# Query and key projections of one attention layer as seven block products in place of eight

## The reference

```
q = hidden_states @ Wq + bq          # (4, 256, 4096): 32 heads of 128
k = hidden_states @ Wk + bk
v = hidden_states @ Wv + bv
q = rms_norm(q, gq); k = rms_norm(k, gk)      # over all 4096 columns
attn = softmax(q k^T / sqrt(128)) per head;  out = attn @ v
return out.reshape(B, S, 4096) @ Wo + bo
```

## Time and profile before

| what | us |
|---|---|
| median of three runs | 2497.82 (2495.07 to 2501.79) |
| the profiled execution | 2499.07 |
| its span, first to last instruction | 2497.3 |
| stage `qk2`, first to last matmul | 1070.01 to 1417.94 |
| attention of layer 2, after the barriers | from 1431.89 |

### The profile page before, as it was taken

One profiled execution on the slowest core, in us unless ns is written; L12 is line 12 of the kernel. 1 busy time (PEld: TensorE's weight loads), 2 busy tenths in 40 slices (PEclk: granted clock), 3 DMA queues, 4 the chain that ended last, 5 costly groups with the idle time before them and its releaser, 6 DMA issues. The chain is left out here.

```text
span 2497.3 us, 37936 instructions
## 1 busy us (share of the span) xinstructions
PE 2393.3 (96%) x12912; PEld 1919.5 (77%) x12912; DVE 1579.3 (63%) x2513; ACT 1102.7 (44%) x2158; POOL 571.3 (23%) x423
## 2 busy tenths in 40 slices
PE   5999999899989899999999999999999999999898
PEld 4777777688866678888888778888888887888666
DVE  5796467754377765544444477777777776543476
ACT  3333146532346432133333366666666654322573
POOL 2132121255231334044444300000000013440000
PEclk8999999999989999999999999999999999999999
DMA  3232174222243222234444422322222222332421
GB/s 88 55 114 83 50 131 89 35 46 45 47 102 67 41 37 41 51 120 141 148 142 147 149 84 77 93 91 86 77 70 86 70 43 36 52 49 42 97 62 45
DMA packets 406196, 195.14 MB, mean 78 GB/s; under 512 B 280393, under 2 KB 359729, under 8 KB 406079
## 3 DMA queue, kind: packets, MB, share of 16 engines
q1 hardware_dynamic: 404860, 191.53, 31.1%
q10 hardware_dynamic: 1218, 2.06, 0.3%
HBM read 129.85 MB, written 44.04 MB: 70 GB/s over the span
## 5 line engine op out<-in xcount | busy, mean ns | idle before, releaser
L616 PE MATMUL banks<-xn_hi,w_hi 128*128 128x512 f32 x1264 | 496.2, 393 | 8.5 <-ACT sgf L1156 5.5
L616 PE MATMUL banks<-xn_lo,w_hi 128*128 128x512 f32 x1264 | 493.0, 390 | 0.0
L616 PE MATMUL banks<-xn_hi,w_lo 128*128 128x512 f32 x1264 | 492.9, 390 | 0.0
L616 PEld LDWEIGHTS banks<-xn_hi,w_hi 128*128 128x128 f32 x1264 | 237.8, 188 | 59.6 <-DVE w_lo L604 5.8
L616 PEld LDWEIGHTS banks<-xn_hi,w_lo 128*128 128x128 f32 x1264 | 237.7, 188 | 49.9
L616 PEld LDWEIGHTS banks<-xn_lo,w_hi 128*128 128x128 f32 x1264 | 237.8, 188 | 48.2
L604 DVE TENSOR_TENSOR w_lo<-tw,w_hi 128x512 fp32r<-128x512 f32 (+2 forms) x136 | 115.1, 853 | 201.9 <-ACT w_hi L596 201.8
L2745 DVE TENSOR_SCALAR raw<-banks,cols 128x512 f32<-128x512 f32 x128 | 103.7, 810 | 180.3 <-ACT sq L2728 180.3
L2757 POOL TENSOR_TENSOR ssq<-ssq,sq 128x512 f32<-128x512 f32 x128 | 165.2, 1290 | 183.2 <-ACT sq L2728 183.2
L1277 POOL TENSOR_TENSOR h_lo<-sgf,h_hi 128x512 fp32r<-128x512 f32 (+1 forms) x94 | 128.1, 1367 | 337.2 <-ACT h_hi L1159 337.2
L476 POOL TENSOR_TENSOR nat<-nat,wscale 128x512 f32<-128x512 f32 (+1 forms) x44 | 52.1, 1188 | 654.2 <-DMA nat<-in_L_ffn_w 654.1
(11 more groups left out here) (290 smaller groups left out, 5550.8 us busy)
## 6 DMA issues: line engine op xcount, KB each, us to landing
qk_scratch<-raw SPq DMA_DIRECT2D x64, 512.0 KB, 3.0
qk_raw<-qk_scratch SPq DMA_DIRECT2D x64, 512.0 KB, 3.8
nat<-in_L_ffn_w SPq DMA_DIRECT2D x48, 256.0 KB
head_scratch<-stage SPq DMA_DIRECT2D x16, 512.0 KB, 3.2
st_qs<-st_hi SPq DMA_DIRECT2D x128, 64.0 KB, 2.0
nat<-in_L_attn_Wq SPq DMA_DIRECT2D x32, 256.0 KB
nat<-in_L_attn_Wk SPq DMA_DIRECT2D x32, 256.0 KB
nat<-in_L_attn_Wv SPq DMA_DIRECT2D x32, 256.0 KB
```

What stands on the lines that cost most here:

```text
L616: mm = nc.tensor.matmul(to[half][:, :], w[0:n, j, k * P:(k + 1) * P], r, start=first and k == 0 and x == 0, stop=last and k == len(rows) - ...
```

## The change

Each head of `qk2` becomes a 2 by 2 block product. The output has block rows q and k of the head (128 each) in the naming of the evacuations; the feature axis is cut in two halves of 256 (KH = 2 tiles), and the tokens in two halves of 512. In the algebra A is the weights' matrix with q's feature halves A11, A12 and k's A21, A22, and B is xn with feature halves 1, 2 and token halves: B11, B12, B21, B22. Seven products of 2 feature tiles by 3 matmuls each (42 matmuls) take the place of eight (48):

```diff
         def sp_qk2(sp, s, opening=False):
...
+            def body(it):
+                for p in range(2):
+                    if not (isinstance(it, int) and it == W_ROUNDS - 1):
+                        sp.wait_ge(lo.sem, s.lo0 + PLAIN + 3 * unit(it, p) + 3)
+                        for x in range(2):
+                            load(4 * it + SLOTS + 2 * p + x, 2 * p + x, head(it, p) + 2)
+                    if has_before(it, p):
+                        was, p_was = unit_before(it, p)
+                        store(2 * p_was + 1, head(was, p_was))
+                    store(2 * p, head(it, p))
...
+        W_A, W_E, W_D = (0, 1), (6, 7), (2, 3)
+
+        def pe_qk2(pe, s):
...
+            def fourth(it, p):
+                pe.wait_ge(raw_done[1].sem, s.raw0[1] + 2 * head(it, p) + 1)
+                multiply(W_A[p], "22", p, 3, False, True).then_inc(product_4.sem, 1)
+
+            def body(it):
+                for p in range(2):
+                    h, n = head(it, p), unit(it, p)
+                    lo_at = s.lo0 + PLAIN + 3 * n
+                    pe.wait_ge(lo.sem, lo_at + 1)
+                    pe.wait_ge(raw_done[1].sem, s.raw0[1] + 2 * h - 2)
+                    multiply(W_A[p], "11", p, "11", True, False).then_inc(product.sem, 1)
+                    pe.wait_ge(lo.sem, lo_at + 3)
+                    pe.wait_ge(raw_done[0].sem, s.raw0[0] + 2 * h - 2)
...
+                    multiply(W_E[p], 0, p, 0, True, False).then_inc(product.sem, 1)
+                    if has_before(it, p):
+                        fourth(*unit_before(it, p))
+                    pe.wait_ge(mid.sem, s.mid0 + 3 * n + 1)
+                    multiply(W_A[p], 1, p, 1, False, False).then_inc(product.sem, 1)
...
+                    multiply(W_D[p], "12", p, "21", True, True).then_inc(product.sem, 1)
+                    pe.wait_ge(mid.sem, s.mid0 + 3 * n + 2)
+                    multiply(W_E[p], 3, p, "22", False, True).then_inc(product.sem, 1)
+                    pe.wait_ge(mid.sem, s.mid0 + 3 * n + 3)
+                    multiply(W_A[p], 2, p, 2, False, False).then_inc(product.sem, 1)
...
+        def act_qk2(act, s):
...
+            def high(it, p):
+                n = unit(it, p)
+                unit_loaded(act, s, it, p)
...
+                    act.wait_ge(product.sem, s.pr0 + 6 * n - 6)
+                nc.scalar.activation(w_hi[:, 2 * p, :], nat[:, 2 * p, :], ACT.Copy).then_inc(hi.sem, 1)
+                if not (isinstance(it, int) and it == 1):
+                    act.wait_ge(product_4.sem, s.p40 + n - 1)
+                nc.scalar.activation(w_hi[:, 2 * p + 1, KH * P:D], nat[:, 2 * p + 1, KH * P:D], ACT.Copy).then_inc(hi.sem, 1)
...
+            def keep(x, to, it, p, done, read):
+                act.wait_ge(product.sem, s.pr0 + done)
+                act.wait_ge(*read)
+                nc.scalar.activation(mids[:, x, :], bank[to[p]][:, :], ACT.Copy).then_inc(mid.sem, 1)
...
+            def body(it):
+                for p in range(2):
...
+                    if has_after(it, p):
+                        high(*after)
+                    keep(0, W_A, it, p, 6 * n + 1, (raw_done[0].sem, s.raw0[0] + 2 * h - 1))
+                    keep(1, W_E, it, p, 6 * n + 2, (raw_done[1].sem, s.raw0[1] + 2 * h - 1))
+                    if has_after(it, p):
+                        high_sums(*after)
+                    if has_before(it, p):
+                        square(*before_, 0)
+                    keep(2, W_A, it, p, 6 * n + 3, (raw_done[0].sem, s.raw0[0] + 2 * h))
+                    if has_before(it, p):
+                        square(*before_, 1)
...
+        def dve_qk2(dve, s):
...
+            def body(it):
+                for p in range(2):
...
+                    if has_before(it, p):
+                        second_k(*before_)
+                    if has_after(it, p):
+                        sums(*after)
+                        low(*after, 0)
+                    if has_before(it, p):
+                        first_k(*before_)
+                    if has_after(it, p):
+                        low(*after, 1)
+                        low(*after, 2)
+                    first_q(it, p)
+                    second_q(it, p)
...
+        def pool_qk2(pool, s):
...
+            def body(it):
+                for p in range(2):
+                    if has_after(it, p):
+                        sums(*unit_after(it, p))
+                    for x in range(2) if has_before(it, p) else ():
+                        add(*unit_before(it, p), x)
...
-                v = qk_raw[:, e % 2, :, :]
-                nc.vector.tensor_tensor(v, v, rms[:, :, at(half)], ALU.mult).then_inc(qk_scaled.sem, 1)
+                for n in range(2):
+                    v = qk_raw[:, e % 2, n, :]
+                    ins = nc.vector.scalar_tensor_tensor(v, v, cols2[:, 3 + n, bass.ds(h, 1)], rms[:, n, at(half)],
+                                                         ALU.mult, ALU.mult)
+                ins.then_inc(qk_scaled.sem, 1)
...
             pool_proj(pool, down2)
+            pool.wait_ge(used.sem, down2.used0)
+            pool_token_sums(pool, qk2)
             pool_qk2(pool, qk2)
```

More of the change, by code:

```diff
@@ new lines, in plan_qk2, with head, unit, unit_after @@
+            s.pr0, s.p40, s.mid0 = product.reserve(6 * units), product_4.reserve(units), mid.reserve(3 * units)
+            return s
+        def head(it, p):
+            return 2 * it + p
+        def unit(it, p):
+            return 2 * it + p - PLAIN // 2
+        def unit_after(it, p):
+            return (it, 1) if p == 0 else (it + 1, 0)
+        def unit_before(it, p):
+            return (it, 0) if p == 1 else (it - 1, 1)
+        def has_before(it, p):
+            return not (isinstance(it, int) and unit(it, p) == 0)
@@ new lines, in has_after, with unit_rounds, unit_weights, unit_loaded @@
+        def has_after(it, p):
+            return not (isinstance(it, int) and head(it, p) == H2 - 1)
+        def unit_rounds(eng, body):
+            body(1)
+            with eng.Fori(2, W_ROUNDS - 1) as it:
+                body(it)
+            body(W_ROUNDS - 1)
+        def unit_weights(p):
+            q, k = nat[:, 2 * p, :], nat[:, 2 * p + 1, :]
+            c1, c2 = slice(0, KH * P), slice(KH * P, D)
+            return q[:, c1], q[:, c2], k[:, c1], k[:, c2]
+        def unit_loaded(eng, s, it, p):
+            for j in (2 * p, 2 * p + 1):
+                eng.wait_ge(loaded[j].sem, loaded_count(s, 4 * it + j, j))
@@ L2733, in dve_qk2_ahead @@
+            act_hi(act, s, LEAD, LEAD, ALL)
+            plain(0)
+            plain(1)
+            high(1, 0)
+            plain(2)
+            high_sums(1, 0)
+            plain(3)
+            unit_rounds(act, body)
+            square(W_ROUNDS - 1, 1, 0)
+            square(W_ROUNDS - 1, 1, 1)
         def dve_qk2_ahead(dve, s, i, j, h):
@@ new lines, in evacuate @@
+            def evacuate(it, p, x, half, to, done, kept):
+                j = 2 * p + x
+                h, n = head(it, p), unit(it, p)
+                dve.wait_ge(product.sem if done else product_4.sem, s.pr0 + 6 * n + done if done else s.p40 + n + 1)
+                if half == x:
+                    dve.wait_ge(stored[j].sem, s.st0[j] + 16 * it)
+                dst, b = raw2[:, j, at(half)], cols2[:, x, bass.ds(h, 1)]
+                if kept is None:
+                    ins = nc.vector.tensor_scalar(dst, bank[to[p]][:, :], b, None, ALU.add)
+                else:
+                    dve.wait_ge(mid.sem, s.mid0 + 3 * n + kept + 1)
+                    ins = nc.vector.scalar_tensor_tensor(dst, bank[to[p]][:, :], b, mids[:, kept, :], ALU.add, ALU.add)
+                ins.then_inc(raw_done[x].sem, 1)
@@ new lines, in xn_parts, with sums, plain @@
+        def xn_parts(part, k, half):
+            return (xn_hi, xn_lo)[part][:, k, at(half)].bitcast(F32)
+        def pool_qk2(pool, s):
+            def sums(it, p):
+                n = unit(it, p)
+                a11, a12, a21, a22 = unit_weights(p)
+                unit_loaded(pool, s, it, p)
+                if not (isinstance(it, int) and it == 1):
+                    pool.wait_ge(product.sem, s.pr0 + 6 * n - 6)
+                nc.gpsimd.tensor_tensor(ws[:, p, 2, :], a11, a21, ALU.subtract).then_inc(ws_pool.sem, 1)
+                nc.gpsimd.tensor_tensor(ws[:, p, 0, :], a21, a22, ALU.add).then_inc(ws_pool.sem, 1)
+            def plain(i):
```

238 lines of the change are left out of this document (198 added, 40 removed).

## The result

The kernel before took 2496.17 us (median of 20 runs, 2493.81 to 2505.16), the changed one 2503.88 us (20 runs, 2497.16 to 2509.44). The ratio is 1.002, with a 95% interval of 1.0012 to 1.0028: **5.0 us slower**, between 3 and 7. (The two medians lie 7.7 us apart and the two means 5.7; the profiled executions differ by 5.0.) That is inside the range of the forecast, but the small number had the wrong sign: I had -1.1 us, and it is +5. The profiled execution took 2504.1 us with a span of 2502.2; the one before had 2499.07 and 2497.3 [table in the profile before].

A forecast was written before the change was run, and what follows sets the result against it. TensorE's matmuls were taken to bound the stage. Terms: -40.8 matmuls, +35.3 wait, +3.4 end, +1 attention, sum -1.1 us; 2498.0 profiled, median 1.3 lower, forecast 2497 us, range 2487 to 2514 (8 in 10).

The forecast's parts named there:

- the small number: Whole program: the forecast's sum of all terms, -1.1 us, called no change.
- The matmuls: Query and key stage: 30 of 32 heads go from 48 to 42 matmuls at 0.227 us each, 40.8 us less.
- one slow matmul behind each: After each stop the second matmul comes 0.34 us behind the first, not 0.23: 0.11 us more per head.
- The wait in its place: TensorE waits after `fourth` for ScalarE's bank A copy, queued behind the 256-wide high part: 28 x 1.26, 35.3 us more.
- the margins: Other engines keep up with a head of 10.78 us, with 0.9, 1.0 and 1.8 us to spare: costed at nothing.
- the covered rival: The gap before bank A's second product is absent or covered: -36 us, 2461 us, chance 8%.
- The end: Stage's end more serial: 4.9 us to the next stage instead of 2.58, `fourth` waits 1.1; together 3.4 us more.
- The sums of the input: GpSimd's 28 sums and 8 copies, at most 46 us, hidden behind the feed-forward's first product, 14 us spare: nothing.
- Scaling in the attention: Attention: one VectorE instruction becomes two, 18 us more engine work, 1 us taken; rival with all 18 showing, 2514 us, 5%.
- VectorE held behind GpSimd: Rival: evacuations with a mid meet GpSimd's adds, `fourth` late: +8 to +26 us, middle 2514 us, chance 10%.
- The forecast's own row: Profile row: a VectorE subtraction with both inputs in SBUF, beside a GpSimd sum, took 1.09 us where 0.69 is usual.
- The clock: Rival: after each gap one product runs at the lower clock level: +40 us, 2537 us, chance 4%.

The follow-up runs named there:

- Experiment 5: Changed kernel with weight and token sums moved 64 to 192 bytes to the plain operands' place within 256 bytes: stage 345.00 us against 348.79, pace 0.2277.
- experiment 6: Kernel before with weights and all behind them moved by 64, 128 or 256 bytes: 2513.05, 2512.96 and 2501.06 us, one run each.
- the last run: Changed kernel with first and third products kept earlier, aligned sums, split ending and GpSimd's weight sums one addition earlier: 2460.19 us, ratio 0.9846.
- Experiment 1: Changed kernel with ScalarE's copy of bank A moved ahead of the second, 256-wide high part: 2474.42 us, ratio 0.9918.
- experiment 8: Changed kernel, Experiment 1's edit plus aligned sums: 2470.59 us; further edits 2474.55, 2471.87, 2460.19. Ring: GpSimd, VectorE and ScalarE queues waiting on each other, 9.9 us a head.
- experiment 7: Changed kernel with the last head's last square and GpSimd's last addition in halves of 512: 3.77 us to the next stage instead of 4.81.

## Why the prediction was right and wrong

**The matmuls.** Right in number (1356), wrong in price. The step that failed is the sentence that "a matmul less is 0.227 us less", read as if the ones that stay kept their pace. They went from 0.2267 to 0.2307: 5.2 of the 5.9 us between the forecast's sum and the trace's. I took the pace from tiles that all lie at one place within 256 bytes and moved it to tiles that don't. Experiment 5 gives 3.9 of the 5.2 us back, and experiment 6 shows the price by itself, 5.7 to 6.6 ns a matmul. The other 1.3 us belong to the stops: I priced one slow matmul behind each (0.34), and experiment 5 shows the rest of two products slower too (0.234 and 0.230). They are gone in the last run, which has no stops (0.2267). A second step failed as well: the stretch behind the stage stood in the sum at nothing and took 1.6 us more, from which goes what I gave too much to the attention (-0.9).

**The wait in its place.** Right, to the hundredth: 1.38 from start to start, 28 times, on ScalarE's copy behind the 256-wide high part. Experiment 1 shows the cause: with the two instructions exchanged the stage is 30.8 us shorter. That it is not 35.4 is the ring of experiment 8, which the stops had hidden. I had put the margins at 0.9 to 1.8 us for a head of 10.78; at 9.52 they don't hold, which is what the covered rival (2461 us) left out. With the ring open the program takes 2460.19; that this is so near 2461 is in part chance, since that run has more edits than the one that takes the stops away.

**The end.** 4.9 forecast, 4.81 in the trace, by the steps as written; `first_k` took 0.75 for the 0.81 that I had.

**The sums of the input.** Hidden. GpSimd's last one ends at 1053.3, and the clearing waits 15.89 us more, where I had 14 to spare:

```profile
1051.83 1.47 POOL L3032 TENSOR_TENSOR xr<-xs,xr_c 128x512 fp32r<-128x512 f32 x1
1069.19 1.81 POOL L3099 MEMSET ssq<- 128x2048 f32 x1 [15.89 <-PE banks L643]
```

**Scaling in the attention.** I took 1 us; it is 0.1 (617.85 and 617.92 from its first matmul to the next norm's). That rival is out.

**VectorE held behind GpSimd.** Not in the changed kernel: its evacuations with bank and tile took 0.75, also beside an addition, and TensorE waited for none but the last. The Trainium skill (SBUF — State Buffer, Who interferes with whom) has VectorE blocked by GpSimd when both its inputs are in SBUF. The forecast's reading of it, that an input in PSUM keeps VectorE free, holds, and the pointer to the bias doesn't spoil it. Where both inputs are in SBUF, the last experiment shows the blocking: 2.61 us for a sum of 0.43, beside an addition of 2.39. That fits the Trainium skill's rule, that such an instruction waits out the whole of GpSimd's, but for 0.15 us: the sum ends 0.28 behind the addition and not 0.43. The forecast's own row is short by the same 0.15 (1.09 for 1.24), so it spoke for the rule more than I read in it.

**The clock.** In the stage it stayed whole, so that rival is out. The Trainium skill (TensorE: Matmul & The Clock Gate, A second HAM failure mode: psum-queue depth-cycling) tells of short idles between groups of matmuls that made the clock oscillate; 28 idles of 1 us did not do so here. What I left at nothing was the stretch behind it: after an idle of 4.4 us and not 2.2, 10.2 us of low clock and not 6.8, +1.6 us. Its cause is open (experiment 7), and one execution of each kernel doesn't show that it is the change's: the kernel before with 256 bytes of offset had the short idle and the same 10.2 us and 13.00.

## What to carry to other kernels

When a change adds buffers for matmuls, look at where they start against the other operand: 64 or 128 bytes off within 256 cost up to 3% of a 512-wide matmul here, a small buffer ahead of them is enough, and the remedy is free. When a stage gets shorter, work out the ring through all queues for the new, shorter period and not for the one with the known stops in it: the order within ScalarE and within GpSimd, with the places of the sums and the split ending, decided between +5 and -37 us for the same arithmetic. A copy that an engine waits for goes ahead of any preparation for the next round in its queue.

## What the hardware showed that I had not expected

- Pace of 512-wide matmuls with a weight load each: 0.2267 us with both operands at the same place within 256 bytes, 0.2333 with 64 bytes between them, 0.2324 with 128, 0.2267 with 256. The values don't matter (0.2307 in three kernels with the same addresses and different values). A slow pair can slow the plain products behind it (0.2315 in place of 0.2267), and after a stop of 1 us the next two products are slower too (0.234 and 0.230 with everything aligned).
- 28 idles of 1 us in 310 us, one every 10.96, left the granted clock whole. After the waits of 2.2 to 5.4 us at the end it stood at its lower level for 6.8, 10.2 or 13.7 us, not in the order of the waits.
- A 256-wide VectorE sum with both inputs in SBUF took 0.43 us alone and 2.60 in the mean beside GpSimd's 1024-wide additions of 2.44.
